# A decoder kernel's cross attention: another order on VectorE, other PSUM banks for the next pair's first projections, and part of the softmax denominators added up on GpSimd

## What is computed

```
q = (x @ Wq).reshape(B, Nq, HEADS, DIM_HEAD)          # 1024 x 8 heads x 64
k = (context @ Wk).reshape(B, Nc, HEADS, DIM_HEAD)    # 6404 x 8 x 64
v = (context @ Wv).reshape(B, Nc, HEADS, DIM_HEAD)
attn = softmax(einsum('bihd,bjhd->bhij', q, k) * SCALE)
out = einsum('bhij,bjhd->bihd', attn, v).reshape(B, Nq, HEADS * DIM_HEAD) @ Wo + bo
```

## Time and profile before

| | us |
|---|---|
| time, median of 3 runs | 1883.76 (1881.23 to 1884.16) |
| the profiled execution: time | 1886.82 |
| its span in the trace | 1885.1 |
| busy: PE, DVE, ACT, POOL | 1557.6, 1368.8, 1122.4, 163.3 |
| pair 0 | 159.1 to 414.6 |
| pair 1 | 414.6 to 666.0 |
| pair 2 | 666.0 to 918.4 |
| pair 3 (no maximum, no items for a next pair) | 918.4 to 1118 |

### The profile page before, as it was taken

The page is one execution under the profiler, slowest core; times in us unless marked ns, Lnnn a source line. Parts: engine busy times, 40 slices in busy tenths (PEclk is TensorE's granted clock), DMA queues, the critical chain, the costliest instruction groups (busy, mean ns, idle before and its releaser), DMA issues.

```text
span 1885.1 us, 25226 instructions
## 1 busy us (share of the span) xinstructions
PE 1557.6 (83%) x8933; PEld 572.4 (30%) x8946; DVE 1368.8 (73%) x2230; ACT 1122.4 (60%) x1479; POOL 163.3 (9%) x104
## 2 busy tenths in 40 slices
PE   2887798998989989999979974999956558978955
PEld 1412233332323323333323221433323412322313
DVE  4697878887888868888868977666633267677774
ACT  4586676766767757767567752555523346656532
POOL 6300000000000000000000003444410000000000
PEclk7857999999999989999989986999978858987977
DMA  4000000000000000000020001111100000000000
GB/s 116 7 1 5 1 1 1 1 1 6 1 1 1 2 2 1 1 1 1 1 54 1 1 1 31 42 43 45 29 0 1 1 0 1 1 1 1 1 1 23
DMA packets 11861, 20.21 MB, mean 11 GB/s; under 512 B 1558, under 2 KB 11046, under 8 KB 11558
## 3 DMA queue, kind: packets, MB, share of 16 engines
q1 hardware_dynamic: 11750, 18.76, 3.7%
HBM read 18.23 MB, written 0.52 MB: 10 GB/s over the span
## 4 chain that ended last, share of the span: by engine, by line
PE 54%; DVE 17%; issue 16%; ACT 7%; POOL 4%; DMA 2%; SPq 0%; POOLq 0%; ACTq 0%; DVEq 0%
PE PS L1639 20%; PE PS L1624 14%; DVE KNB L1002 4%; POOL WRK L526 4%; PE PS L1669 4%; PE PS L1587 3%; ACT WRK L669 2%; PE PS L1514 2%; ACT KNB L689 2%; DVE QS L1056 1%; DVE WRK L1050 1%; PE PS L1506 1%; DMA KNB<-in_ctx_fm_dram 1%; PE PS L1893 1%; DVE KB L932 1%
## 5 line engine op out<-in xcount | busy, mean ns | idle before, releaser
L1050 DVE TENSOR_TENSOR WRK<-WRK 128x1024 f32<-128x1024 f32 x500 | 611.4, 1223 | 64.2 <-ACT WRK L669 38.9
L669 ACT ACTIVATE WRK<-PS 128x1024 f32<-128x1024 f32 (+1 forms) x510 | 497.3, 1022 | 110.2 <-PE PS L1624 101.9
L1639 PE MATMUL PS<-WRK,V 128*64 128x512 f32 (+1 forms) x2040 | 500.6, 611 | 0.0
L1002 DVE CUSTOM_DVE_ANT_0 KNB<-PS,KNB 128x512 f16<-128x512 f32 (+2 forms) x464 | 330.2, 729 | 113.1 <-PE PS L1669 100.1
L689 ACT ACTIVATE KNB<-PS 128x512 f16<-128x512 f32 (+2 forms) x306 | 180.7, 591 | 149.9 <-PE PS L1669 149.8
L1771 PE MATMUL PS<-WRK,KNB 128*128 128x512 f16 x828 | 200.2, 389 | 29.2 <-DVE KNB L932 11.5
L1624 PE MATMUL PS<-Q,KB 64*128 64x512 f16 (+1 forms) x1428 | 193.4, 382 | 11.8 <-ACT WRK L669 11.6
L1639 PEld LDWEIGHTS PS<-WRK,V 128*64 128x64 f32 (+1 forms) x2040 | 125.0, 137 | 250.7 <-issue 182.3
L1624 PE MATMUL PS<-KNB,KB 64*128 64x512 f16 (+1 forms) x1224 | 154.5, 379 | 0.0
L1771 PEld LDWEIGHTS PS<-WRK,KNB 128*128 128x128 f16 x828 | 78.6, 99 | 142.5 <-issue 34.6
L650 ACT ACTIVATE KNB<-PS 128x1024 f16<-128x1024 f32 x96 | 98.0, 1024 | 26.7 <-DVE MXP L1002 15.7
(11 more groups left out here) (322 smaller groups left out, 1556.6 us busy)
## 6 DMA issues: line engine op xcount, KB each, us to landing
V<-in_moe_w_dram SPq DMA_DIRECT2D x44, 192.0 KB, 2.3
KNB<-in_ctx_fm_dram SPq DMA_DIRECT2D x1, 2401.5 KB, 18.7
CTX<-in_ctx_fm_dram SPq DMA_DIRECT2D x1, 2401.5 KB, 13.4
BW<-in_bit_w_dram SPq DMA_DIRECT2D x1, 960.0 KB, 8.2
PWK<-in_pair_w_dram SPq DMA_DIRECT2D x4, 192.0 KB, 3.1
SM<-in_small_dram SPq DMA_DIRECT2D x1, 716.5 KB, 4.3
XT<-in_x_fm_dram SPq DMA_DIRECT2D x1, 512.0 KB, 5.2
X<-in_x_tm_dram SPq DMA_DIRECT2D x1, 512.0 KB, 8.0
```

Of the source, the lines that this page charges most:

```text
L669: e.activation(PR[0:r, u % 2, b, :], bank(2 * b, 2 * b + 2, slice(0, r)), ACT.Exp).then_inc(S("exp"), 1)
L1002: return e.tensor_tensor_reduce(diffs, sums, diffs, 0.5, NEG, ALU.add, ALU.max, accum_out=out)
L1050: e.tensor_tensor(ACC[0:r, hf % 2, :], ACC[0:r, hf % 2, :], part, ALU.add).then_inc(S("acc"), 1)
L1639: ins = e.matmul(PS[h * HD:(h + 1) * HD, 4, :], v(r, j, h), PR[0:r, unit_no(hf, i) % 2, b, h * HALF:(h + 1) * HALF], start=(j == 0), stop= ...
```

## The change

Four edits; the new `add_up` in the diff stands in POOL's list. `add_up` on VectorE takes columns 0 to 767 only in halves 0 to 5 (pairs 0 to 2); POOL does the same addition for columns 768 to 1023, tile by tile, and ACT (before it overwrites PR) and TensorE (before it sums ACC) wait for both. In a slot VectorE adds tile 0 before `first` and tile 1 before `mid`, where it did `first`, tile 0, `mid`, tile 1. The second q projection moves from slot 1 to slot 0. And q's two parts and the first kd and ks of a pair go to banks 6 and 7, outside of BANK5's sequence: kd and ks then wait for the copies of q, and q for nothing new. POOL's all-reduce for the ternary sums moves behind the adds of unit 8.

```diff
+SHARE = 3 * T // 4
+def dve_part(hf):
+    return SHARE if hf < 2 * (PAIRS - 1) else T
...
-        at[0] += [("wk", n), ("q", (n, 0))]
-        at[1] += [("wv", n), ("q", (n, 1)), ("kd", (n, 0)), ("ks", (n, 0))]
+        at[0] += [("wk", n), ("q", (n, 0)), ("q", (n, 1))]
+        at[1] += [("wv", n), ("kd", (n, 0)), ("ks", (n, 0))]
...
+BANK_OF = {("q", 0): 6, ("q", 1): 7, ("kd", 0): 6, ("ks", 0): 7}
+def bank_of(x):
+    return BANK_OF.get((x[0], x[1][1]), 5) if x[0] in ("q", "kd", "ks") else 5
+BANK5 = [x for p in range(PAIRS) for s in range(SLOTS) for x in ITEMS[p][s] if x[0] in FREED_BY and bank_of(x) == 5]
...
+            def add_up(hf, i, b):
+                n, r = tile_no(hf, i, b), rows_of(2 * i + b)
+                part = PR[0:r, unit_no(hf, i) % 2, b, SHARE:T]
+                e.wait_ge(S("exp"), n + 1)
+                if i == 0 and b == 0:
+                    if hf >= 2:
+                        e.wait_ge(S("den_ps"), hf - 1)
+                    e.tensor_copy(ACC[:, hf % 2, SHARE:T], part).then_inc(S("acc_pool"), 1)
+                else:
+                    e.wait_ge(S("acc_pool"), n)
+                    total = ACC[0:r, hf % 2, SHARE:T]
+                    e.tensor_tensor(total, total, part, ALU.add).then_inc(S("acc_pool"), 1)
...
                     e.wait_ge(S("acc"), tile_no(hf2, i2, min(b, tiles_of(i2)[-1])) + 1)
+                    if dve_part(hf2) < T:
+                        e.wait_ge(S("acc_pool"), tile_no(hf2, i2, min(b, tiles_of(i2)[-1])) + 1)
...
-                    maximum(p, first)
                     if before[0] >= 0:
                         add_up(*before, 0)
-                    maximum(p, mid)
+                    maximum(p, first)
                     if before[0] >= 0 and len(tiles_of(before[1])) > 1:
                         add_up(*before, 1)
+                    maximum(p, mid)
                     maximum(p, last)
...
-                if order[x]:
+                if bank_of(x) == 5 and order[x]:
                     name, count = freed(BANK5[order[x] - 1])
                     e.wait_ge(S(name), count)
+                elif bank_of(x) > 5 and kind != "q":
+                    e.wait_ge(S("q_lo"), 2 * a[0] + (1 if kind == "kd" else 2))
```

More of the change, by code:

```diff
@@ L135 @@
 FREED_BY = {"v": "v_ev", "q": "q_lo", "kd": "k16", "ks": "k16", "dk": "k_lo", "den": "den_r", "wo": "r_add"}
-BANK5 = [x for p in range(PAIRS) for s in range(SLOTS) for x in ITEMS[p][s] if x[0] in FREED_BY]
+BANK_OF = {("q", 0): 6, ("q", 1): 7, ("kd", 0): 6, ("ks", 0): 7}
+def bank_of(x):
+    return BANK_OF.get((x[0], x[1][1]), 5) if x[0] in ("q", "kd", "ks") else 5
+BANK5 = [x for p in range(PAIRS) for s in range(SLOTS) for x in ITEMS[p][s] if x[0] in FREED_BY and bank_of(x) == 5]
 def freed(x):
@@ L509, in _ @@
             e.partition_all_reduce(AM[:, 0:1], AX[:, 0:1], P, RED.max).then_inc(S("am"), 1)
-            e.wait_ge(S("bit_rows"), 1)
-            e.partition_all_reduce(BT[:, 0:7], BR[:, 0:7], P, RED.add).then_inc(S("bit_sum"), 1)
+            def add_up(hf, i, b):
[10 more added lines that the diff above has]
+                    e.tensor_tensor(total, total, part, ALU.add).then_inc(S("acc_pool"), 1)
+            for hf in range(2 * (PAIRS - 1)):
+                for i in range(NU):
+                    for b in tiles_of(i):
+                        add_up(hf, i, b)
+                    if hf == 0 and i == 8:
+                        e.wait_ge(S("bit_rows"), 1)
+                        e.partition_all_reduce(BT[:, 0:7], BR[:, 0:7], P, RED.add).then_inc(S("bit_sum"), 1)
             for i in range(1, 3):
@@ L698, in bank5 @@
                 elif kind == "q":
-                    q_out(*a, 5)
+                    q_out(*a, bank_of(x))
                 elif kind in ("kd", "ks"):
-                    k16_out(*a, int(kind == "ks"), 5)
+                    k16_out(*a, int(kind == "ks"), bank_of(x))
                 elif kind == "dk":
@@ L1041, in add_up @@
                 n, r = tile_no(hf, i, b), rows_of(2 * i + b)
-                part = PR[0:r, unit_no(hf, i) % 2, b, :]
+                w = dve_part(hf)
+                part = PR[0:r, unit_no(hf, i) % 2, b, 0:w]
                 e.wait_ge(S("exp"), n + 1)
@@ L1046, in add_up @@
                         e.wait_ge(S("den_ps"), hf - 1)
-                    e.tensor_copy(ACC[:, hf % 2, :], part).then_inc(S("acc"), 1)
+                    e.tensor_copy(ACC[:, hf % 2, 0:w], part).then_inc(S("acc"), 1)
                 else:
                     e.wait_ge(S("acc"), n)
-                    e.tensor_tensor(ACC[0:r, hf % 2, :], ACC[0:r, hf % 2, :], part, ALU.add).then_inc(S("acc"), 1)
+                    total = ACC[0:r, hf % 2, 0:w]
+                    e.tensor_tensor(total, total, part, ALU.add).then_inc(S("acc"), 1)
             def reciprocals(hf, k):
@@ L1647, in denominators @@
                 e.wait_ge(S("acc"), (hf + 1) * KT)
+                if dve_part(hf) < T:
+                    e.wait_ge(S("acc_pool"), (hf + 1) * KT)
                 for h in range(2):
@@ L1693, in bank5 @@
                     return
-                if order[x]:
+                if bank_of(x) == 5 and order[x]:
                     name, count = freed(BANK5[order[x] - 1])
                     e.wait_ge(S(name), count)
+                elif bank_of(x) > 5 and kind != "q":
+                    e.wait_ge(S("q_lo"), 2 * a[0] + (1 if kind == "kd" else 2))
                 if kind == "q":
-                    q_in(*a, 5)
+                    q_in(*a, bank_of(x))
                 elif kind in ("kd", "ks"):
-                    k16_in(*a, int(kind == "ks"), 5)
+                    k16_in(*a, int(kind == "ks"), bank_of(x))
                 elif kind == "dk":
```

## The result

The changed kernel takes 1849.66 us in the median (1849.08 to 1854.33); the kernel before, run beside it, 1882.91 us. The ratio is 0.9829, with a 95% interval of 0.9811 to 0.9848. It is faster by 33 us. The forecast was 1870 us, 13 us faster: the time lies in the range, but the gain is two and a half times the one forecast.

The account below looks back on a forecast made before the run. First halves were held bound by the loop maximum, two adds, maximum. Terms -18.4 - 13.5 + 16.5 + 2.0 = -13.4 us took the profiled 1886.82 to 1873.4, median forecast 1870 us, range 1845 to 1890 us.

Parts of the forecast that it names:

- What bounds the kernel, and the loops: First halves: the loop maximum, two adds, maximum binds; after the change plain slots take TensorE's 3.70 us, kd and ks 4.24.
- The order in first halves: Add, max, add, max there gains 5.7 us each in pairs 1 and 2, 7.0 in pair 0, sum 18.4 us.
- my five runs: Five sequences of kd, ks and plain slot in a first half, 0.93 us gained in each, 4.7 us together.
- no gain by itself: POOL's quarter saves 0.27 us in 306 VectorE adds, counting only where a loop with an add ends last.
- The order in second halves: The add ahead of the maximum loses 0.5 us behind each of 12 key projections; 5.5 us a half, 16.5 in all.
- are hidden already: Second halves: the slot shown takes 4.45 us, all of it TensorE's, so the adds cost nothing there before the change.
- Banks 6 and 7: Pair starts: 5.5 us gained each in pairs 1 and 2, 2.5 in pair 0; sum 13.5 us, bounds 3 and 19.
- Shared reads: Adds of VectorE and POOL that both read SBUF hold each other up; charged 2 us in all.
- slower at 1895 us: Rival, 18%: POOL adds delay VectorE's adds in slots behind key projections, 25 us more over 36 slots.
- POOL's all-reduce: Moved behind the adds of unit 8, costed at nothing because VectorE asks for it only in slot 12.
- the gain is kept in the second halves: Rival, 27%: ACT's copy ends earlier or the next slot is as tight as now; 16.5 us come back, 1854 us.
- T+4.0: End of ACT's copy in a key projection's slot, counted from TensorE's first maximum; VectorE's split starts then.

Follow-up runs that it names:

- e2: Banks 6 and 7 with both q projections in one slot, old order, no POOL share, against the kernel before: 1863.8 us, ratio 0.990.
- e4: POOL's quarter of the adds alone, with order and banks of before, against the kernel before: 1869.8 us, ratio 0.993.
- e6: The changed kernel with the old order throughout, keeping POOL's quarter and the banks: 1846.9 us, ratio 0.980 to the kernel before.
- e7: The changed kernel with the old order only in the slot behind a key projection: 1843.4 us, ratio 0.979 to the kernel before.
- e10: The kernel of e9 with each POOL add replaced by a memset that reads no SBUF: 1835.7 us, ratio 0.975 to the kernel before.
- e8: The changed kernel with POOL's quarter only from half 1 on, its all-reduce ahead of all its adds: 1843.3 us, ratio 0.979 to the kernel before.
- e3: The new order alone, old banks and slots, VectorE adding all 1024 columns, against the kernel before: 1884.6 us, ratio 1.000.
- e5: The changed kernel with the old order (maximum, add, add) in second halves only: 1840.7 us, ratio 0.979 to the kernel before.
- e9: The changed kernel with POOL's quarter from half 1 on and the old order in second halves: 1835.8 us, ratio 0.975 to the kernel before.
- e11: The kernel of e9 with half of the columns on POOL instead of a quarter: 1833.7 us, ratio 0.974 to the kernel before.

## Why the prediction was wrong, step by step

- **What bounds the kernel, and the loops.** Right, to the hundredth: plain slots are 3.70 us apart in the changed kernel, kd and ks slots 4.24.
- **The order in first halves.** I summed order and quarter to 5.7 us in pair 1. Measured is 15.3 - 7.6 (the banks, e2) = 7.7 us. Two microseconds short; the three slots at the reciprocals took 14.9 us instead of 16.0, where I had 0.5 us lost, and the rest is one plain slot, which gains 0.67 us, that my five runs left out. In pair 0 I had 7.0 us; 6.0 - 5.4 = 0.6 came, and the missing part is the all-reduce's (below).
- **Which edit earns it.** I called the quarter "no gain by itself" and gave the plain slots' 0.67 us to the order. With the old order the quarter alone brings plain slots to 3.83 us and 14 us in all (e4), and quarter and banks without the new order are not slower than the whole change (e6). The sum of the two was near in first halves, its split between them was not.
- **The order in second halves: the step that failed most.** I had a loss of 5.5 us each, 16.5 us in all; the measured loss is 1.2 us each, 3.7 us. The mechanism is there (0.38 us a slot instead of my 0.5, and e7 shows that these slots hold 2.9 us), but two things were mis-sized. I charged it in 12 slots; 2.9 us are six waits of 0.38 us and one of 0.6 in slot 50. Behind the early key projections in slots 30 to 33, and behind the one in slot 41, which has three steps, nothing is lost. And I left out that shorter adds help a second half by themselves: 1.9 us in e4. So the order costs 3.15 us and the quarter gives 1.9. I had looked only for its harm because the adds "are hidden already" there; they were not hidden at the reciprocals and the slots of three steps.
- **Banks 6 and 7.** 13.5 us forecast for the pairs' starts, 7.6 + 8.6 + 5.4 = 21.6 us measured (e2). Pair 2 gains a microsecond more than pair 1 because its start had taken 19.4 us, at a granted clock of 0.74, where pair 1's took 18.4. My count of the steps gave 6.6 us with slot 2 at 11.75 us; it came at 10.8. I then took 1.1 us off in case the clock fell again; it did not fall. In pair 0 I guessed 2.5 without a count and 5.4 came; 4.5 of that are its start, where slot 2 came 10.4 us after the seeds instead of 14.9.
- **Shared reads.** 2 us charged, none measured (e10). The rule of the Trainium skill (SBUF — State Buffer, "Who interferes with whom") is borne out by durations: adds of both engines wait for each other. The rival built on it, slower at 1895 us, had its mechanism and not its price: the mean delay is 0.05 us an add, where it needed 0.37 in the slots behind a key projection; the add in that place in the slot shown, at 569.06, took 0.95 us, so it didn't wait at all.
- **POOL's all-reduce.** Costed at nothing, it cost 6.7 us in pair 0 (e8), and some 9 us in e7's profiled execution, where the same code took 127.5 us. I checked when VectorE asks for its result, and not what stands behind it on POOL: the adds of the units that follow, for which ACT waits. This error alone goes the other way; e8, without it, gains 39 us.

The sum against the two profiled executions (1886.82 and 1849.08 us): pairs' starts and first halves -37.6 us (I had -31.9), second halves +3.7 (+16.5), shared reads 0 (+2), -3.3 us ahead of pair 0, where the code is unchanged and where the first seeds stand between 153.6 and 158.8 us in the experiments' profiles, +1.6 in pair 3 and -2.2 behind it. What happened behind pair 2 no run explains; it was not forecast either. The rival "the gain is kept in the second halves" (1854 us) came nearest in its number, but not for its reason: it wanted ACT's copy earlier than T+4.0, and the copy ended at T+4.0 to the hundredth (568.42, with the slot's first maximum at 564.42). Second halves lost less because fewer slots wait and because the quarter helps them.

## What to carry to other kernels

An order that suits one phase of a loop can harm the next: the new order alone gains 4 to 6 us in each first half and loses 4.7 in each second, and as one edit it measures as nothing (e3). With the quarter there it gains 1.3 to 3.5 us and loses 3.15 (e5, e6). Look at which wait ends last in each phase and choose by phase. And when an instruction is given work of a new kind between its old work, look at both sides of the old instruction on its own engine, not only at who waits for it.

## What the runs showed of the hardware that I had not expected

POOL spent 5.8 to 6.2 us of issue ahead of an all-reduce that follows adds, and 6.9 to 7.4 us ahead of the first adds that follow an all-reduce, in each of the five kernels that mix them in pair 0's first half. The way back to a plain tensor_tensor costs as much as the way there. The copy of 256 columns ahead of the adds started without such a gap, and so did e10's memsets, which stand where the adds stood. In the changed kernel each of the gaps begins with a pair of MODIFY_POOL_CONFIG instructions on POOL's sequencer, and e10 has none ahead of its memsets. The Trainium skill (GPSIMD Engine Reference, "2.1 Instruction dispatch") has about 6 us for the first call of a freshly loaded kernel. The trace agrees in the size and in the instruction that comes first (5.7 us from it to the all-reduce, 7.0 and 7.2 us to the adds); that code is loaded in this time no run shows. In e8, e9 and e11 the gap (6.9 to 7.4 us) falls at the start of pair 0's second half, which is 0.3 to 1.0 us longer there than the later ones; in e10 it isn't.

A VectorE add with both inputs in SBUF and a POOL add exclude each other: 768 columns take 0.95 us beside a POOL that only writes and up to 1.52 us otherwise, 256 columns on POOL 0.71 to 1.36 us. With two adds of each in a slot of 3.7 us that cost the kernel no time that can be measured (e9 and e10).
